# Attention of a graph and transformer network: the sums of the probabilities inverted as ten columns by way of DRAM, the product with the inverse on GpSimd, the low halves of the probabilities on VectorE a tile late

## The reference

```python
x1 = layernorm(x, ln1_g, ln1_b)
q, k, v = x1 @ wq, x1 @ wk, x1 @ wv            # 8 heads of 64; L3 adds bq, bk, bv
scores = einsum('bqhd,bkhd->bhqk', q, k) * 64 ** -0.5
p = softmax(scores, axis=-1)                   # exp(s - max) / sum
x = x + einsum('bhqk,bkhd->bqhd', p, v).reshape(B, S, H) @ wo      # L3 adds bo
```

## Time and profile before

| | us |
|---|---|
| median of 3 runs | 3995.57 |
| the three runs | 3989.58, 3996.42, 3995.57 |
| time of the profiled execution | 3993.08 |
| its span | 3991.4 |
| attention of L0, from the first low half (995.4) to the next product (1424.8) | 429 |
| the same in L3 (3255.6 to the end of `finish`, 3691.0) | 435 |

### The profile page before, as it was taken

How to read it: one execution, slowest core, us unless ns; L and a number is a source line. 1 busy time by engine, 2 the same in 40 slices (tenths; PEclk the granted TensorE clock), 3 DMA queues, 4 the chain that set the end, 5 groups by cost and what they waited for, 6 DMA issues and landing times. The chain is left out here.

```text
span 3991.4 us, 43842 instructions
## 1 busy us (share of the span) xinstructions
PE 2938.3 (74%) x13239; PEld 2075.3 (52%) x13240; DVE 1734.2 (43%) x3263; ACT 992.4 (25%) x2149; POOL 645.2 (16%) x375
## 2 busy tenths in 40 slices
PE   5888649966888872998578588956865578887735
PEld 3555526545766742665264366644634456766523
DVE  6677651134677622333524511031132357666323
ACT  1222320103665620111201211110111245665100
POOL 0000000000554512111100000000010024555032
PEclk9999869987998875999788799968977788898766
DMA  6000360210000014886420300005321100000154
GB/s 240 0 0 0 71 204 1 50 47 8 6 5 3 0 29 146 289 297 210 117 105 2 84 0 11 0 25 169 99 76 32 50 11 3 5 3 0 26 166 130
DMA packets 129057, 271.56 MB, mean 68 GB/s; under 512 B 40666, under 2 KB 41898, under 8 KB 127667
## 3 DMA queue, kind: packets, MB, share of 16 engines
q1 hardware_dynamic: 52723, 132.58, 11.2%
q10 hardware_dynamic: 46848, 92.38, 7.0%
q0 software_dynamic: 29376, 45.16, 3.8%
HBM read 190.83 MB, written 79.14 MB: 68 GB/s over the span
## 5 line engine op out<-in xcount | busy, mean ns | idle before, releaser
L947 POOL TENSOR_TENSOR probs_lo<-x,probs_hi 125x1250 fp32r<-125x1250 f32 x160 | 460.1, 2878 | 1692.9 <-ACT x L919 1498.3
L1001 DVE TENSOR_REDUCE mx<-ps 125x1 f32<-125x500 f32 (+1 forms) x480 | 271.0, 587 | 128.1 <-PE ps L792 115.0
L917 ACT ACTIVATE probs_hi<-ps 125x500 fp32r<-125x500 f32 (+1 forms) x480 | 254.0, 529 | 248.0 <-PE ps L801 245.3
L243 PE MATMUL ps<-onehot_src,onehot_dst 125*128 x1200 | 259.4, 355 | 42.0 <-DVE onehot_dst L219 15.2
L218 DVE TENSOR_SCALAR onehot_src<-iota,src_f 125x1250 f16 x400 | 218.0, 545 | 114.1 <-PE ps L243 101.8
L792 PE MATMUL ps<-K_hi_lo,Q_hi_twice 128*125 128x500 f32 (+1 forms) x480 | 198.9, 421 | 83.4 <-DVE mx L1001 74.7
L919 ACT ACTIVATE x<-ps 125x500 f32<-125x500 f32 (+1 forms) x480 | 255.9, 533 | 0.0
L1488 DVE COPY yb<-ps 78x512 f32<-78x512 f32 (+1 forms) x100 | 68.3, 688 | 357.3 <-PE ps L1423 253.6
L1423 PE MATMUL ps<-w2s,hT 128*78 128x512 f32 (+1 forms) x480 | 220.4, 606 | 3.2 <-ACT hT L1448 3.2
L800 PE MATMUL ps<-Q_hi_twice,K_hi_lo 128*125 128x500 f32 (+1 forms) x480 | 197.2, 411 | 33.6 <-DVE Q_hi_twice L980 15.3
L243 PEld LDWEIGHTS ps<-onehot_src,onehot_dst 125*128 x1200 | 121.5, 102 | 173.6 <-issue 119.3
(11 more groups left out here) (351 smaller groups left out, 5391.8 us busy)
## 6 DMA issues: line engine op xcount, KB each, us to landing
room<-in_L_ffn_w_p ACTq DMA_DIRECT2D x72, 512.0 KB, 5.5
w2s<-in_L_ffn_w ACTq DMA_DIRECT2D x72, 512.0 KB, 6.7
buf<-zeros SPq DMA_DIRECT2D x37, 512.0 KB
slabs<-ah_spill SPq DMA_DIRECT2D x20, 585.9 KB
xb<-buf SPq DMA_DIRECT2D x64, 156.0 KB
yb<-yb POOLq DMA_DIRECT2D x64, 156.0 KB, 7.0
xb<-buf SPq DMA_DIRECT2D x36, 250.0 KB
tv<-in_L_ffn_tv_W_p SPq DMA_DIRECT2D x2, 4096.0 KB
```

What stands on the lines that cost most here:

```text
L243: mm_ = pe.matmul(ps[:, 3 * half + c, 0:cn], ohd[:, slot, :].rearrange("p o n -> p (o n)"), ohs[:, slot, c0:c0 + cn].rearrange("p o n -> p ...
L917: act.activation(PH[:, t % 2, c0:c0 + cn], ps[0:P, ST + n, 0:cn], ACT.Exp, scale=SCALE).then_inc(p_hi, 1)
L947: pool.tensor_tensor(PL[:, t % 2, :], PT[:, t % 2, :], PH[:, t % 2, :].bitcast(fp32), ALU.subtract)\
L1001: v.tensor_reduce(mx[:, t, n:n + 1], ps[0:P, SQ + cc % 2, 0:cn], AX.X, ALU.max)\
```

## The change

`remainder` moves from POOL to DVE. There it stands behind the maxima of tile t and makes the low half of tile t-1; that of tile 9 comes in `between`, behind `negate`. `finish` is gone. In its place SP sends one row of the sums to DRAM and reads it back as 125 partitions x 10 columns; DVE inverts those 10 columns (`invert`, in tile 2 of the next head); SP stores them, and reads the row back into 64 partitions, in two loads of 600 and 650 columns; POOL makes the product (`normalise`, two instructions). Behind the last head the same chain runs with nothing beside it.

The inverse takes the place of other tiles in SBUF, and so `biased` moves to the space of `x`. ACT's and SP's writes to that space now wait for the store of `x`, whose end the first `norm_rows` no longer waits for, though it is still issued ahead of the small loads on SP's queue (`later`). `wo` and `bo` are loaded in `attention`, behind the weights of head 0. All this holds for both transformers. There are five semaphores more in each.

```diff
-def loads_beside(block, sem, pairs):
+def loads_beside(block, sem, pairs, later=()):
     if pairs:
         @block.sync
         def _(sp):
+            for dst, src, done in later:
+                sp.dma_start(dst, src).then_inc(done, 16)
             for dst, src in pairs:
                 sp.dma_start(dst, src).then_inc(sem, 16)
             sp.wait_ge(sem, 16 * len(pairs))
...
+                def turn_sums(h):
+
+                    sp.wait_ge(ctx_out, h * 3 + 4)
+                    sp.dma_start(sums_dram[0:1, :], cu[DH:DH + 1, :]).then_inc(sums_in, 16)
+                    sp.wait_ge(sums_in, h * 32 + 16)
+                    sp.dma_start(sums[:, 0, :], sums_dram[0, :].rearrange("(p q) -> p q", p=P)).then_inc(sums_in, 16)
+                    sp.wait_ge(inv_ready, h + 1)
+                    sp.dma_start(sums_dram[1, :].rearrange("(p q) -> p q", p=P), sums[:, 1, :]).then_inc(inv_in, 16)
+                    sp.wait_ge(inv_in, h * 48 + 16)
+                    for c0, cn, inv in INV:
+                        sp.dma_start(inv[:, :], sums_dram[1, c0:c0 + cn].partition_broadcast(DH)).then_inc(inv_in, 16)
+
                 load_weights(0, 1)
-                with sp.Fori(1, H) as h:
-                    load_weights(h, h + 1)
+                sp.wait_ge(spare_free, 32)
+                for dst, src in late_loads:
+                    sp.dma_start(dst, src).then_inc(late_in, 16)
+                load_weights(1, 2)
+                load_weights(2, 3)
+                with sp.Fori(0, H - 3) as h:
+                    load_weights(h + 3, h + 4)
+                    turn_sums(h)
+                with sp.Fori(H - 3, H) as h:
+                    turn_sums(h)
...
-                    act.wait_ge(norm_out, h * HALF + 1)
+                    act.wait_ge(norm_out, h * 2 + 2)
...
-                def remainder(h, t):
-                    pool.wait_ge(p_out, h * 30 + (3 * t + 3))
-                    pool.wait_ge(lo_done, h * T + (t + 1))
-                    pool.tensor_tensor(PL[:, t % 2, :], PT[:, t % 2, :], PH[:, t % 2, :].bitcast(fp32), ALU.subtract)\
-                        .then_inc(p_lo, 1)
-
-                with pool.Fori(0, H) as h:
-                    for t in range(T):
-                        remainder(h, t)
+                def normalise(h, j, chunk):
+
+                    pool.wait_ge(inv_in, h * 48 + 48)
+                    pool.sem_inc(cu_ready, 1)
+                    for c0, cn, inv in INV:
+                        pool.tensor_tensor(ctxT[DH * j:DH * j + DH, chunk, c0:c0 + cn].rearrange("p o n -> p (o n)"),
+                                           cu[0:DH, c0:c0 + cn], inv[:, :], ALU.mult).then_inc(norm_out, 1)
+                    pool.wait_ge(norm_out, h * 2 + 4)
...
+                def remainder(h, t):
+                    v.wait_ge(p_out, h * 30 + (3 * t + 3))
+                    v.wait_ge(lo_done, h * T + (t + 1))
+                    v.tensor_tensor(PL[:, t % 2, :], PT[:, t % 2, :], PH[:, t % 2, :].bitcast(fp32), ALU.subtract)\
+                        .then_inc(p_lo, 1)
...
-                def finish(h, j, chunk, m):
-
-                    if m == 0:
-                        v.wait_ge(ctx_out, h * 3 + 4)
-                    c0 = PIECE * m
-                    v.reciprocal(inv[:, m % 2, :], cu[DH:128, c0:c0 + PIECE]).then_inc(inv_ready, 1)
-                    v.wait_ge(inv_ready, h * HALF + (m + 1))
-                    v.tensor_tensor(ctxT[DH * j:DH * j + DH, chunk, c0:c0 + PIECE].rearrange("p o n -> p (o n)"),
-                                    cu[0:DH, c0:c0 + PIECE], inv[:, m % 2, :], ALU.mult).then_inc(norm_out, 1)
+                def invert(h):
+
+                    v.wait_ge(sums_in, h * 32 + 32)
+                    v.reciprocal(sums[:, 1, :], sums[:, 0, :]).then_inc(inv_ready, 1)
...
                         if has_next:
                             maxima(h + 1, t)
-                        if last and t < HALF:
-                            finish(*last[0], t)
+                        if t:
+                            remainder(h, t - 1)
+                        if last and t == 2:
+                            invert(*last[0])
                         if t == HALF and has_second:
                             split_lo(h + 2)
...
                         negate(h + 1)
+                    remainder(h, T - 1)
+                    if has_next:
                         v.wait_ge(lo_done, h * T + (T + 2))
                         take_v(h + 1)
```

More of the change, by code:

```diff
@@ L347, in in_two, with norm_rows @@
     return [(dst[0:120], src[0:120]), (dst[120:P], src[120:P])]
-def norm_rows(nc, k, x, xn, xT=None, affine=None, eps=1e-5, beside=(), have_stats=False):
+def norm_rows(nc, k, x, xn, xT=None, affine=None, eps=1e-5, beside=(), have_stats=False, later=()):
     with ExitStack() as ctx:
@@ L369, in norm_rows @@
         with nc.Block() as block:
-            loads_beside(block, loaded, beside)
+            loads_beside(block, loaded, beside, later)
             @block.vector
@@ L716, in attention @@
         cu = room(128, (N,))
-        inv = room(DH, (2, PIECE))
+        sums = sb("sums", [P, 2, T])
+        INV = ((0, 600, room(DH, (600,))), (600, N - 600, sb("inv", [DH, N - 600])[:, :]))
         mx, mr, negm = sb("mx", [P, T, 3]), sb("mr", [P, T]), sb("negm", [P, T + 1], f32r)
@@ L941, in _, with tiles, between @@
             def _(pool):
-                pool.sem_inc(p_lo, 2)
-                def remainder(h, t):
-                    pool.wait_ge(p_out, h * 30 + (3 * t + 3))
-                    pool.wait_ge(lo_done, h * T + (t + 1))
-                    pool.tensor_tensor(PL[:, t % 2, :], PT[:, t % 2, :], PH[:, t % 2, :].bitcast(fp32), ALU.subtract)\
-                        .then_inc(p_lo, 1)
-                with pool.Fori(0, H) as h:
-                    for t in range(T):
-                        remainder(h, t)
+                pool.sem_inc(norm_out, 2)
+                def normalise(h, j, chunk):
[5 more added lines that the diff above has]
+                    pool.wait_ge(norm_out, h * 2 + 4)
+                last = []
+                def tiles(h, j, those, has_next, has_second):
+                    if last and HALF - 1 in those:
+                        normalise(*last[0])
+                def between(h, j, chunk, has_next, has_second):
+                    last[:] = [(h, j, chunk)]
+                schedule(pool, tiles, between)
+                normalise(*last[0])
             @block.vector
@@ L1037, in between @@
                         take_projections(h + 2, j)
-                    last[:] = [(h, j, chunk)]
+                    last[:] = [(h,)]
                 take_v(0)
@@ L1048, in _ @@
                 schedule(v, tiles, between)
-                for m in range(HALF):
-                    finish(*last[0], m)
+                invert(*last[0])
 def route(nc, k, yT, wr, br, E_, topk, cap, keep_last, r):
@@ L1556, with __init__ @@
 class Room:
-    def __init__(self, tile):
-        self.flat, self.used = tile[:, :, :].rearrange("p a b -> p (a b)"), 0
+    def __init__(self, tile, used=0):
+        self.flat, self.used = tile[:, :, :].rearrange("p a b -> p (a b)"), used
     def __call__(self, partitions, shape):
@@ L1629, in transformer @@
         g1, b1, g2, b2 = (sb(ctx, n, [128, C]) for n in ("g1", "b1", "g2", "b2"))
-        norm_rows(nc, k, x, res, have_stats=True, beside=in_two(rowtiles(x_spill), x) + [(g1[:, :], a[pre + "ln1_g_c"]), (b1[:, :], a[pre + "ln1_b_c"]),
+        norm_rows(nc, k, x, res, have_stats=True, later=[(to, what, x_out) for to, what in in_two(rowtiles(x_spill), x)],
+                  beside=[(g1[:, :], a[pre + "ln1_g_c"]), (b1[:, :], a[pre + "ln1_b_c"]),
                                          (g2[:, :], a[pre + "ln2_g_c"]), (b2[:, :], a[pre + "ln2_b_c"])])
```

30 lines of the change are left out of this document (18 added, 12 removed).

## The result

| | before | after |
|---|---|---|
| median, us (first comparison, 4 runs each) | 3992.57 | 3860.82 |
| lowest and highest run | 3984.45, 3996.42 | 3854.78, 3863.34 |
| span of the profiled execution | 3991.4 | 3857.9 |
| attention, both layers, from the first weight load to the next product | 975.0 | 848.3 |
| the rest of the span | 3016.4 | 3009.6 |

The ratio of the medians is 0.967, with a 95% interval of 0.965 to 0.9691: 131.7 us less. The forecast was 3889, 105 less, with 3862 as the low end of the range.

The account below looks back on a forecast made before the run. TensorE was taken to bound late tiles and VectorE early ones, its product held by GpSimd's subtraction. 112 + 5 - 3 - 12 - 3 + 3 + 3 = 105 us gained, so 3889 us, range 3862 to 3924.

Parts of the forecast that it names:

- Part 1: Heads 1 to 6: `finish` leaves VectorE, twelve stretches go from 41.0 to 31.7 us; 112 us gained, 108 to 120.
- Part 4: GpSimd's product in tile 4 makes VectorE's subtractions wait; 1.0 us in 12 heads, 12 us lost, 0 to 29.
- part 3: Low half of the weights, tile 5: 5 us gained in the heads 0, 3 us lost behind maxima and subtraction.
- Part 2: Steady tiles: the subtraction, 1461 ns on VectorE, fits into its 1.53 us of idle time; cost 0.
- Rival B: VectorE becomes the bound in every tile, 3.67 us instead of 3.44; 29 us, total 3918; chance 0.13.
- Part 5: Sums by way of DRAM: covered inside heads, 12.8 us against 11.24 behind the last head; 3 us lost.
- Part 6: Between heads: 14 gaps x 0.2, 3 us gained; last head's final low half 1.4 us earlier, twice, 3 us gained.
- Part 7: Loads and stores: small columns still issued behind the store of `x`, so 0; otherwise 4.6 in each of two, 9 us.
- A: Store of `x` leaves the path and products fall between subtractions; 9 and 12 us more, total 3868; chance 0.08.
- C: Nothing gained: work only exchanged, VectorE and GpSimd still hold each other; total 3988; chance 0.04.
- D: Slower: VectorE's subtraction takes GpSimd's 2.88 us as ScalarE writes the same tiles; 146 us, total 4034; chance 0.05.

Follow-up runs that it names:

- tiny_product: Changed kernel with GpSimd's two products cut from 600 and 650 columns to 8 each; 3847.18 us, ratio 0.9634 to the kernel before.
- invert_t4: Changed kernel with the sums inverted behind tile 4's subtraction instead of tile 2's; 3854.49 us, ratio 0.9678 to the kernel before.
- extra_big: Changed kernel with one more VectorE maximum, over 500 columns and read by nobody, in each tile of heads with a successor; 3884.33 us, ratio 0.9746.
- lo_only: Kernel before with only the low halves moved to VectorE, `finish` unchanged; 3945.4 us, ratio 0.9892.
- after: The changed kernel itself, as first compared and profiled against the kernel before; 3860.82 us, ratio 0.967.
- after_again: The changed kernel run once more, nothing altered; 3854.25 us, ratio 0.9665 to the kernel before.
- store_behind: Changed kernel with the store of `x` issued behind the row norm's four small loads instead of ahead; 3836.52 us, ratio 0.9614 to the kernel before.

## Where the prediction held, and the steps that failed

The mechanism was right: VectorE without `finish` no longer holds the early tiles, and its subtraction fits beside TensorE. What failed are two terms of the sum. Part 1 put all twelve heads at the granted clock of 0.93 of head 0, and only four of them had it after the change; that gave 9.2 us more. Part 4, with part 3, put the wait for GpSimd's product and the low half of the weights at 14.5 us, and they cost about 6. Together these are the 17.7 us of heads 1 to 6. Another 4.9 us of the miss lie in the rest of attention, and the others outside it, where no run explains them.

**What bounds the kernel, and part 1.** Right: without `finish` every tile steps at TensorE's 3.44, and the waits for maxima went from 74.7 to 6.1 us. The term was taken too small, though the measure of it was right. I took 31.7 us for the stretch because "each head starts with some microseconds at the lower clock", a clock of 0.93. With the 16.3 us between the stretches (198.2 / 12 less 0.2) that makes 48.0 a head, and the heads without a collision on the path take 47.9 at 0.93 (`tiny_product`, `invert_t4`). But after, only four of twelve have that clock. Taking all twelve at their 48.50 would give 582.0 us; they took 572.8. That is **9.2** of the 17.7 us, a term the sum didn't have: the granted clock isn't the same before and after. Before had 0.88 in eight of these heads and 0.91 or 0.94 in the others. That the heads came out at the better clock was luck as far as the forecast goes, and it hangs together with parts 3 and 4: with the collision gone, eleven of twelve had 0.93, and the heads took 575.0 instead of 572.8 (`tiny_product`). So 9.2 and 8.5 are shares of a sum and not two effects that could be had one without the other.

**Part 2.** Right at 0, and far safer than "the cover is thin" said. The subtraction kept its 1.45. What was wrong in it was the start of 0.15 us that I added to each instruction. It came from the end of a reciprocal to the product that needs its result; instructions that don't need each other overlap by 0.08 instead. Maxima and subtraction back to back take 1.50 + 1.37 = 2.87 and not 3.3: `extra_big` put 0.66 more into each tile, and the steady step stayed at 3.44 to 3.45. Rival B rested on the same sum and was given 0.13.

**Parts 3 and 4.** Forecast 12 x 1.0 and 10 x 0.25 in heads 1 to 6, measured 0.57 in the ten with weights to split (0.54 and 0.03) and 0.03 in the two without: about 6 instead of 14.5, so **8.5** of the 17.7 us. Two things were wrong in it. The products fell beside the subtractions in tiles 4 and 5, not in tile 4 alone, and in the first of the two it was GpSimd that waited; I had put all of the waiting on VectorE. And the second lost only what GpSimd still had to do, 0.54 of 1.59. It showed on the path only because the low half of the weights stands behind it in tile 5; in tile 7 it is free (`invert_t4`). The range of part 4, 0 to 29, held it.

**Part 5.** Forecast 3 lost, measured 0.9. The sum of the way was near: 1350.47 to 1361.86 is 11.4, against 12.8 forecast; up to the next product (1362.36) it is 11.9, where before took 11.24. The pieces were not: two stores 1.26 and 1.46 (2.2 each in the sum), the load 1.5 (2.6), but 4.2 for the two loads that each spread one row over 64 partitions, counted as 2.7. The estimate from the fixed cost of about 2.0 us in the Trainium skill (DMA: Bandwidth & Descriptors, Anatomy of one DMA) was 11.1. The total agrees with that to 0.3, the single pieces, 1.26 to 4.2, don't.

**Part 6.** The last low half came earlier, head 7 gained 4.0 where 3 was forecast with its gap. Between the other heads a gain of 0.2 can't be told apart from the clock. The head that this part and rows 4 and 5 call head 2 is head 3 in the count from 0; nothing hangs on it.

**Part 7.** Right at 0: the first row norm took 17.55 us after and 17.57 before. What it would be worth if the order were turned was put at 4.6 a layer, from SyncE's wait less the time of a load; turned, it gave 11.1 in the row norm and about 10.4 up to the first weight load. The wait of 6.8 in rows 11 was only the part that SyncE spent waiting; it had spent much of the rest issuing the four loads behind the store (2.11 us for the first, at 864.88 in the trace of after, and 0.36 where it stands ahead).

**The rivals.** A's time, 3868, was nearest, but not for its reasons: the store did not leave the path, and the products met the subtractions. C and D fell: the product 0.41 beside an idle GpSimd, the subtraction 1.45 with ScalarE writing. For C stood the sentence of the Trainium skill (Perfetto Trace Analysis, Optimizing Scalar/DVE Operations) that moving work between these two engines "might not help". Here the move helped: VectorE does in 1.45 what GpSimd does in 2.88, and by itself it was worth 32.4 us of attention (`lo_only`).

**The range.** Its low end was built from A's two terms. The larger of the two unforeseen gains, the clock, had no term and so no bound, though the trace of before shows it differ from one head to the next (0.88 to 0.94). As the trace of after shows, a head at 1.00 takes 2.7 less than one at 0.93; with half of that as a bound, 12 x 1.35 = 16 us, the range would have begun at 3846.

## What to carry to other kernels

When two engines hold each other up, count who starts first: the later one pays only what the earlier one has left, and an engine with slack gives it back over the next tiles. Before calling an engine full, probe it: one instruction a tile whose result nobody reads shows the slack that recorded durations hide (0.57 us here, where 0.07 was read). Then a delay can be priced, since only what exceeds the slack reaches the step. Where a tuned loop is bound by TensorE, look for the waits after which its granted clock falls; one 0.4 us copy moved ahead was worth 23 us here, part of it by the shorter wait (0.9 us a head in L0) and part where the clock then stayed up. And where a block waits for small loads, look at what stands ahead of them in the queue: a store moved behind four of them was worth 18 us.

## What the runs showed of the hardware

- VectorE's recorded durations overlap in a row: 1.58, 0.66 and 1.45 us of work start 3.45 apart, about 0.08 an instruction (`extra_big`).
- With GpSimd and VectorE on SBUF tiles together, the one that starts later is stretched by what is left of the other: GpSimd's 1.24 to 2.37, VectorE's 1.45 to 1.99.
- The granted clock falls to 0.50 behind a wait of 1.7 to 1.8 us at the head's start in most heads and doesn't in some. In three traces with the changed kernel's attention (`after`, `after_again`, `store_behind`) these are the same heads and the same clocks, but for one head of twelve at 0.93 in one trace and 0.96 in two; in the two traces of before four of twelve differ. With a collision of 0.54 us gone elsewhere in the head, eleven heads of twelve had 0.93 instead of four. A head with 6.8 us at 0.50 took 2.7 us more than the one that stayed at 1.00. Why it falls in one head and not in another is open.
- Two small loads that each spread one row, of 600 and 650 numbers, over 64 partitions took 4.2 us until their reader started, the two issued 0.5 apart, where a load of 125 x 10 took 1.5 and stores 1.26 and 1.46.
- A small load issued behind a store of 2.5 MB takes SyncE 1.8 to 2.4 us to issue (`after`), 0.36 to 0.43 ahead of it (`store_behind`).
